# Attention over 16 groups: row maxima computed three items ahead instead of five and spread differently over the key tiles, the second column-sum pass one key tile earlier, the inversion moved in front of the split

## What is computed

```
x = x + tanh(g_xattn[0]) * fake_quant(layernorm(x)) @ fake_quant(ctx)
x = x + tanh(g_ffn[0])   * (per_token_quant(layernorm(x)) @ dequant(W_int).T + bias)
x = x + tanh(g_xattn[1]) * attention(layernorm(x), ctx, ctx; Wq, Wk, Wv, Wo)
x = x + tanh(g_ffn[1])   * layernorm(x) @ dequant_fp4(packed).T
```

```
q = (query @ Wq) ... 32 heads;  k, v = (ctx @ Wk), (ctx @ Wv) ... 8 heads, each repeated 4 times
scores = einsum('bhqd,bhkd->bhqk', q, k) * 32 ** -0.5
probs  = softmax(scores, axis=-1)
out    = einsum('bhqk,bhkd->bhqd', probs, v);  return out @ Wo
```

## Time and profile before

| what | value |
|---|---|
| median of 3 runs | 996.39 us (995.18 to 996.71) |
| the profiled execution | 997.46 us, its span 995.7 us |
| mean granted clock of the matrix engine | 0.97 of full speed |
| PE busy | 882.3 us (89%) |
| DVE busy | 670.0 us (67%) |
| POOL busy | 526.8 us (53%) |
| ACT busy | 422.6 us (42%) |

### The profile page before, as it was taken

One profiled execution on the slowest core, in us unless ns is written; L12 is line 12 of the kernel. 1 busy time (PEld: TensorE's weight loads), 2 busy tenths in 40 slices (PEclk: granted clock), 3 DMA queues, 4 the chain that ended last, 5 costly groups with the idle time before them and its releaser, 6 DMA issues.

```text
span 995.7 us, 15794 instructions
## 1 busy us (share of the span) xinstructions
PE 882.3 (89%) x4784; PEld 354.3 (36%) x4784; DVE 670.0 (67%) x974; ACT 422.6 (42%) x730; POOL 526.8 (53%) x236
## 2 busy tenths in 40 slices
PE   3988899868789987998898899888988998999998
PEld 2655655324345433222222222222222221344443
DVE  4788867999875488677777777777777771155532
ACT  3333323422312212566666676666666667110100
POOL 4222354494310045477878787777787878421210
PEclk9999999879899989899999999999999999999999
DMA  5953212012021555155534453454344523412241
GB/s 176 336 170 129 69 56 65 0 51 68 10 95 44 153 135 140 29 114 115 114 82 85 105 114 82 103 114 108 81 85 109 109 56 78 85 36 50 48 132 74
DMA packets 68857, 94.69 MB, mean 95 GB/s; under 512 B 33360, under 2 KB 53840, under 8 KB 64720
## 3 DMA queue, kind: packets, MB, share of 16 engines
q1 hardware_dynamic: 64208, 60.58, 20.2%
q0 software_dynamic: 4608, 33.56, 16.6%
HBM read 41.55 MB, written 12.58 MB: 54 GB/s over the span
## 4 chain that ended last, share of the span: by engine, by line
PE 58%; DVE 20%; DVEq 7%; issue 6%; ACT 4%; DMA 2%; SPq 1%; POOL 0%; POOLq 0%; ACTq 0%
PE sbank L1418 10%; PE sbank L1427 10%; PE mpair L1369 8%; DVEq L778 7%; DVE mx L1062 6%; PE sbank L1214 3%; PE sbank L1215 3%; PE sbank L1216 3%; PE sbank L1437 3%; PE sbank L1505 3%; PE sbank L1522 3%; PE sbank L1507 3%; PE sbank L1509 3%; PE sbank L1520 3%; ACT regC L724 3%
## 5 line engine op out<-in xcount | busy, mean ns | idle before, releaser
L1062 DVE TENSOR_REDUCE mx<-mpair 128x1 f32<-128x1024 f32 (+1 forms) x256 | 302.5, 1216 | 107.1 <-PE mpair L1369 105.3
L724 ACT ACTIVATE regC<-sbank 128x512 f32<-128x512 f32 x512 | 281.1, 595 | 161.0 <-PE sbank L1418 158.6
L1369 PE MATMUL mpair<-regD 96*128 96x512 f16 x512 | 168.1, 388 | 43.7 <-DVE mx L1062 39.1
L1418 PE MATMUL sbank<-regD 98*128 98x512 f16 x512 | 185.0, 387 | 6.9 <-ACT regC L724 3.4
L483 POOL TENSOR_TENSOR wraw<-regC 128x2048 f32<-128x2048 f32 x32 | 145.2, 4536 | 26.3 <-ACT regC L724 25.8
L1427 PE MATMUL sbank<-regC,regD 128*32 128x512 f32 x1024 | 136.9, 607 | 1.0 <-ACT regC L724 1.0
L1418 PEld LDWEIGHTS sbank<-regD 98*128 98x128 f16 x512 | 46.6, 97 | 193.1 <-ACT regC L724 161.4
L483 POOL TENSOR_TENSOR regD<-regC 128x2048 f32<-128x2048 f32 x16 | 72.6, 4537 | 27.6 <-PE sbank L1437 15.3
L1369 PEld LDWEIGHTS mpair<-regD 96*128 96x128 f16 (+1 forms) x512 | 48.9, 99 | 107.1 <-DVE mx L1062 56.8
L483 POOL TENSOR_TENSOR tail<-regC 128x2048 f32<-128x2048 f32 x16 | 72.9, 4556 | 5.6 <-PE sbank L1437 5.6
L428 POOL TENSOR_SCALAR wraw<-wraw 128x1024 f32<-128x1024 f32 x16 | 17.6, 1101 | 89.2 <-ACT regR L662 81.0
(11 more groups left out here) (160 smaller groups left out, 1367.6 us busy)
## 6 DMA issues: line engine op xcount, KB each, us to landing
regD<-wraw POOLq DMA_DIRECT2D x16, 1024.0 KB, 7.0
tail<-wraw POOLq DMA_DIRECT2D x16, 1024.0 KB, 7.3
xT_lo<-in_ctx SPq DMA_DIRECT2D x16, 512.0 KB, 5.5
wraw<-in_L_ffn_W_int SPq DMA_DIRECT2D x8, 512.0 KB, 6.7
wraw<-in_L_xattn_Wq SPq DMA_DIRECT2D x8, 512.0 KB, 3.3
regD<-q_hi_scratch SPq DMA_DIRECT2D x32, 128.0 KB, 2.4
wraw<-in_L_xattn_Wo SPq DMA_DIRECT2D x8, 512.0 KB, 3.4
out<-X SPq DMA_DIRECT2D x16, 256.0 KB, 2.0
```

What stands on the lines that cost most here:

```text
L724: nc.scalar.activation(probs[:, kt % 4, h, :], bank[4 + h % 2], ACT.Exp, scale=SCALE).then_inc(s["exp_ok"], 1)
L1062: v.tensor_reduce(mx[m][:, bass.ds(n, 1)] if par is not None else mx[m][:, n:n + 1], slot[:, :, :], AX.XY, ALU.max).then_inc(s["mx_red"], 1)
L1369: m = pe.matmul(mpair[slot][:, half, :], qst[par][0:96, bass.ds(n * P, P)], kst[par][0:96, half * 512:(half + 1) * 512], start=True, stop= ...
L1418: pe.matmul(bank[4 + h % 2], kst[par][0:98, kt * P:(kt + 1) * P], qst[par][0:98, h * 512:(h + 1) * 512], start=True, stop=True).then_inc(s ...
```

## The change

The items that are computed two groups ahead become 3 instead of 5 (`LEAD`), so that items 3 to 15 of group g + 1 and then items 0 to 2 of group g + 2 stand in a group. `counts` changes from 2, 1, 2, 1+2, 2, 1, 2, 1+2 items in key tiles 0 to 7 to 1+2, 2, 1+2, 2, 2, 1, 2, 1. The second `sum_half` moves from key tile 5 to key tile 4. On DVE the two steps of `invert` move from behind items 0 and 1 of the far group to behind items 14 and 15 of the next group, the second of them ahead of `split_max`.

```diff
         ITEMS = S * REP // P
-        LEAD = 5
+        LEAD = 3
...
                 for n in range(LEAD, ITEMS):
                     if ahead >= 1:
                         reduce_item(g + 1, nxt, n)
+                    if not first and n >= ITEMS - 2:
+                        invert(g - 1, n - ITEMS + 2)
                 if ahead >= 1:
                     split_max(g + 1, cur, g // 3 + 1)
                 for n in range(LEAD):
-                    if not first and n in (1, 2):
-                        invert(g - 1, n - 1)
                     if ahead >= 2:
                         reduce_item(g + 2, far, n)
...
-                counts = [(0, 2), (0, 1), (0, 2), (1, 2), (0, 2), (0, 1), (0, 2), (1, 2)]
+                counts = [(1, 2), (0, 2), (1, 2), (0, 2), (0, 2), (0, 1), (0, 2), (0, 1)]
...
                     half(kt, 1)
-                    if kt in (1, 5) and not first:
-                        sum_half(g - 1, kt // 5, isinstance(g, int) and g == 1)
+                    if kt in (1, 4) and not first:
+                        sum_half(g - 1, kt // 4, isinstance(g, int) and g == 1)
```

## The result

The changed kernel takes 981.64 us (median of 4 runs, 979.97 to 983.46) against 996.55 for the kernel before (4 runs). The ratio is 0.985, 95% interval 0.9827 to 0.9873: 14.9 us faster where 22.8 were forecast.

What follows compares the result with a forecast made beforehand. PE sets the period, with 3.17 us of waiting a group. A gain of 1.65 us a group over 13 groups (21.5), plus 1.0 and 0.3 outside, takes 996.39 to 973.6 us; own range 970 to 978, wider range 969 to 986.

Steps and rivals of the forecast that it cites:

- eight stretches: A group's PE time cut at `pv` starts, second half of one key tile plus first half of the next; forecast 26.82 us together.
- The stalls of the earlier trace in stretches 2, 6 and 7: PE waiting for DVE in the kernel before: 0.79, 0.80 and 1.30 us a group.
- The new stall ahead of `turn_max`: Stretch 5: without the sum, `turn_max` waits for item 15's reduction; 1.08 us of new stall, stretch stays at 3.63.
- The split's delay: Stretch 6: inversion ahead of the split makes item 0 wait some 0.17 us; times count from T6, that stretch's `pv` start.
- Rival C: Stretch 1's margins of 0.3 us are used up and its third item waits 0.79 a group: 984 us, chance 0.13.
- with the end of the fold: The maxima rows' DMAs land with the fold issued ahead of them; 4.99 us from issue to score isn't their own latency.
- rival A: Maxima rows have their own latency, 4.99 us from issue, costing 1.5 of 1.65 us gained a group: 992 us, chance 0.12.
- Stretch 7: Last stretch of a group: two items and no inversion in DVE's way, so 2.88 us.
- No stall, by 0.26 us: Next group's first score: can start at 12.26 us behind key tile 4's `pv`, wanted at 12.52, so no wait for maxima rows.
- rivals A and B: Late maxima rows: A by fixed latency; B by a loaded queue, score stalled 3.3 us a group, 1016 us, B's chance 0.09.
- Group 0 with the lead-in: Start of the attention, outside the 13 like groups: taken as -1.0 us, between -2.5 and +0.5.
- group 14: Next-to-last group: stretch 1 longer, stretch 2 shorter, moved sum hidden in the wait for the rows; -0.3 us.

Runs made afterwards that it cites:

- e2: Kernel before with only the second sum moved to key tile 4 and the inversion moved ahead of the split, old LEAD and counts: 996.06 us, ratio 0.9999.
- e6: e3 with `turn_max` behind the `pv` matmuls of key tile 6 in place of ahead of them: 973.37 us, ratio 0.9785.
- e4: Changed kernel folding only two of four heads, exponentials taken of a sixty-fourth of the scores: 975.75 us, ratio 0.9812.
- e3: Changed kernel with LEAD 4 in place of 3, two items in key tile 7 and none in key tile 0's first half: 975.58 us, ratio 0.9808.
- e1: Kernel before with only LEAD = 3 and the new counts, sum and inversion left in place: 981.55 us, ratio 0.9854.
- e5: Kernel before with LEAD 6, other counts, `turn_max` in key tile 5, second sum in 4, inversion behind far items 0 and 3: 966.12 us, ratio 0.9711.
- e8: e5 with the first step of the inversion ahead of item 0 of the far group in place of behind it: 967.32 us, ratio 0.9713.

## Why the prediction was right in its way, and its gain 8 us too high

The time, 981.64, lies in the stated range (969 to 986) but 8 us above the 973.6 of the sum and outside the forecast's own 970 to 978.

Right, point by point. Six of eight stretches came to 0.01, and stretch 6 to 0.04. The stalls of the earlier trace rows in stretches 2, 6 and 7 went. The new stall ahead of `turn_max`, read from group 0, came as forecast: the move of the sum earned nothing (e2), and e6 shows that it is one chain with the split behind it. Its length was read from a row and held, but not what it was put down to: the work of that stretch was taken as 2.44 + 0.11, and e6 shows 2.88 with no transpose in it, so part of the "stall" is ACT. The split's delay was 0.21 where 0.17 stood (T6 + 1.36 less T6 + 1.23 is 0.13). Rival C did not occur: item 8 did not wait. The reading of "with the end of the fold" was right: in the changed kernel the rows are issued 1.5 us later against the fold and still land behind it, in 3.0 where it was 4.6, and e4 settles it against rival A. The strongly ordered increments that the prediction cited from the Trainium skill (DMA: Bandwidth & Descriptors, section "Queues, rings and completion order") agree with these landings: 4.6 and 3.0 behind the whole fold, 1.7 behind half of it.

The forecast gain was 22.8 us, the spans moved by 14.0. Where the other 8.8 went:

1. Stretch 7, "item 2, then item 3 of the next group, no inversion in DVE's way: 2.88": the step looked at DVE alone, not at ACT. The order of one item in each half runs into ACT's 1.08 us a bank. 3.10 instead of 2.88, 13 x 0.22 = 2.9 us. Shown by e3.
2. "No stall, by 0.26 us": true in 11 of 13 groups (the rows of group 7 had landed 0.6 ahead of the score). In groups 1 and 5 the second row came late and the score waited, 1.44 and 1.22 us more. Around group 5 the timeline reads:

```profile
560.02 0.88 POOL L490 DMA_DIRECT2D regD<-wraw  x1 [0.59 <-POOL wraw L483]
...
564.11 1.82 SPq L344 DMA_DIRECT2D regD<-mT  x2
...
569.18 0.39 PE L1418 MATMUL sbank<-regD 98*128 98x512 f16 x1 [1.31 <-DMA regD<-mT]
```

The fold landed at 567.0, the first row at 567.2, the second at 569.1. In the microsecond from 566 the DMA queues show a transfer of the instruction queue:

```profile
q8 instruction: 1, 0.02, 7.6%
```

Such a load falls ahead of the late row in group 1 and group 5 of the changed kernel, of e1, e3 and e4 alike, and in the other groups of the changed kernel the rows are on time. The kernel before had the late row too (the 6.2 of the earlier trace rows, in group 1), where it met no score. That the instruction load causes the delay is inferred from these coincidences and not shown: no kernel was made without it, and in group 5 of the kernel before such a load falls at 569.4, just ahead of the second row, which lands on time at 570.2 (4.4 behind its issue).
3. The wait of group 1 was followed by a slower clock, which cost stretch 0 of group 2 another 1.31. PE had been idle for 1.51 us before it; the granted clock (1.00 is 2.4 GHz, 0.50 is 1.2 GHz) fell a microsecond after work had begun again:

```profile
458.40:459.40 1.00, 0.99 (x6) 0.33 (x7) 0.00 (x0) 0.39 (x1) 1.00 (x1) 1.00 0.00 0
459.40:461.00 1.60, 1.60 (x9) 0.18 (x8) 1.22 (x1) 0.69 (x2) 1.60 (x1) 0.51 0.00 0
461.00:463.00 2.00, 2.00 (x9) 0.68 (x6) 0.00 (x0) 1.34 (x3) 1.41 (x2) 0.53 0.15 45
```

No term of the sum stood for it, and rivals A and B lacked it too. The length of the wait alone doesn't foretell it: group 5's 1.31 left the clock at 1.00, and so did 1.78 in e5 and 2.05 in e8 (last section).
4. Group 0 with the lead-in brought 0.4 where 1.0 was taken, and group 14 lost 0.15 where 0.3 was to be gained: 1.0 together.
5. 1.1 us were lost ahead of the attention, where both kernels have the same code: PE's first matmuls of group 1 began at 394.3 before and at 395.4 after. In the other runs this point lies between 391.2 and 394.7, so it is scatter, which a comparison of two profiled executions contains.

These add up to 2.9 + 2.7 + 1.3 + 1.0 + 1.1 = 9.0; the 0.2 too much is the balance of small terms. Stretch 6 took 0.04 more than forecast and stretches 1, 4 and 5 took 0.01 less, in each group, and in the kernel before stretch 7 of groups 6 and 9 was 0.2 longer than in the others. So the mechanism was right and terms were mis-sized: above all the margins at the first score. By e1 and e2 the account can also be written so: the spread is worth 14.5 us alone, the other half of the change nothing alone. What the second half does beside the spread is to lengthen stretch 4 by 1.05 us in each group, which puts the score behind the rows: the waits for them go in 11 of the 13 groups (nine were about 0.9 us in e1), at the price of a stretch as long.

## What to carry to other kernels

When a piece of work is moved out of a stretch, look for the wait that it covered there; e2 shows a move that gives and takes to the hundredth. Before a consumer is moved up, list everything that its operands stand behind: here a 4 KB DMA issued 2 to 4 us behind a 1 MB DMA landed only with it, and the kernel that issues it first (e5, which also spreads the items differently) gained twice what the change did. A margin of 0.3 us on a path that other queues touch isn't a margin: price the late case too, with the clock that may fall behind the wait (here 1.3 us for one wait of 1.51). And when an engine is seen to be late, look whether it was busy or itself waiting (e8) before calling it the bound.

## What the hardware showed that I had not expected

The same 4 KB DMA took 1.7 us alone, 3.0 or 4.6 behind a fold that had been running for 4.1 or 2.6 us, and 1.7 again behind a fold of half the size. The half fold took 4.5 us where the whole one took 7.0; if its time is a fixed part and one that goes with the bytes, the fixed part is, by these two, about 2 us (an estimate). And the granted clock of the matrix engine fell to half behind single idle times of 1.51 us (changed kernel), 1.68, 1.70, 2.69 and 2.77 (e1) and 1.94 (e8), and stayed at 1.00 behind others of 0.9 (e1, nine groups), 1.31 (changed kernel), 1.78 (e5) and 2.05 (e8). Two of these are from one run, e8: behind the longer wait, in group 6, the clock stayed, and behind the shorter, in group 14, it fell.

```profile
565.36 0.88 PE L1418 MATMUL sbank<-regD 98*128 98x512 f16 x2 [2.05 <-ACT regC L724]
...
774.16 0.88 PE L1418 MATMUL sbank<-regD 98*128 98x512 f16 x2 [1.94 <-ACT regC L724]
```
